# A GRU step on one core: candidate scan into PSUM, bank zeroings in steps of their own, keep's high products later

## What is computed

```python
def step(hprev, gxt):
    gh = hprev @ whh.T + bhh
    r = jax.nn.sigmoid(gxt[:, :h] + gh[:, :h])
    z = jax.nn.sigmoid(gxt[:, h:2 * h] + gh[:, h:2 * h])
    n = jnp.tanh(gxt[:, 2 * h:] + r * gh[:, 2 * h:])
    hn = (1.0 - z) * n + z * hprev
    return (hn, hn)
...
fwd = _bigru(x_inner, f_wih_fw, f_whh_fw, f_bih_fw, f_bhh_fw, f_wih_rv, f_whh_rv, f_bih_rv, f_bhh_rv)
bwd = jnp.flip(_bigru(jnp.flip(x_inner, 1), b_wih_fw, b_whh_fw, b_bih_fw, b_bhh_fw, b_wih_rv, b_whh_rv, b_bih_rv, b_bhh_rv), 1)
y = jax.nn.silu(fwd + bwd) * jax.nn.silu(z)
```

## Time and profile before

| | |
|---|---|
| median of 3 runs | 1226.55 us (1225.07 to 1228.66) |
| the profiled execution | 1223.94 us |
| its span | 1222.1 us |
| steps of L2, first to last reset product of `h_hi` | 296.4 to 722.0 us |
| PE, DVE, ACT busy | 1081.0, 943.3, 777.5 us |
| mean granted TensorE clock | 0.585 |
| ACT zeroings of a bank half | 120 of `reset_sum`, 120 of `keep_sum` in both layers |

### The profile page before, as it was taken

How to read it: one execution, slowest core, us unless ns; L and a number is a source line. 1 busy time by engine, 2 the same in 40 slices (tenths; PEclk the granted TensorE clock), 3 DMA queues, 4 the chain that set the end, 5 groups by cost and what they waited for, 6 DMA issues and landing times. The chain is left out here.

```text
span 1222.1 us, 57375 instructions
## 1 busy us (share of the span) xinstructions
PE 1081.0 (88%) x22390; PEld 854.9 (70%) x22390; DVE 943.3 (77%) x5701; ACT 777.5 (64%) x4509; POOL 113.1 (9%) x94
## 2 busy tenths in 40 slices
PE   3787799858999999999999968999999999999996
PEld 2555254344888888888888855688888888888885
DVE  3544799984888888888888885688888888888886
ACT  4224620007777777777777764777777777777773
POOL 1001389910000000000000000000000000000000
PEclk8588899957555555555555557555555555555555
DMA  4000500000000000000000000000000000000000
GB/s 119 2 1 12 131 1 1 1 5 2 4 4 4 4 4 4 4 4 4 3 4 4 4 3 5 3 4 4 3 4 4 4 4 3 4 4 4 4 3 27
DMA packets 8234, 12.71 MB, mean 10 GB/s; under 512 B 5745, under 2 KB 7121, under 8 KB 7674
## 3 DMA queue, kind: packets, MB, share of 16 engines
q1 hardware_dynamic: 7962, 9.05, 2.9%
HBM read 8.26 MB, written 0.79 MB: 7 GB/s over the span
## 5 line engine op out<-in xcount | busy, mean ns | idle before, releaser
L1037 DVE TENSOR_TENSOR_SCAN L2s_h_hi<-L2s_renew,L2s_terms 96x32 f16<-96x32 f32 x512 | 112.9, 221 | 74.4 <-ACT L2s_terms L1081 16.0
L1037 DVE TENSOR_TENSOR_SCAN L3s_h_hi<-L3s_renew,L3s_terms 96x32 f16<-96x32 f32 x512 | 113.0, 221 | 74.4 <-ACT L3s_terms L1081 16.0
L1129 PE MATMUL L2s_reset_sum<-L2s_h_hi,L_w_hidden 97*128 97x8 f16 x2048 | 141.0, 179 | 20.8 <-DVE L2s_h_hi L1037 8.4
L1129 PE MATMUL L3s_reset_sum<-L3s_h_hi,L_w_hidden 97*128 97x8 f16 x2048 | 141.1, 179 | 20.6 <-DVE L3s_h_hi L1037 7.8
L1129 PEld LDWEIGHTS L3s_reset_sum<-L3s_h_hi,L_w_hidden 97*128 97x128 f16 x2048 | 94.6, 107 | 78.6 <-DVE L3s_h_hi L1037 31.5
L1129 PEld LDWEIGHTS L2s_reset_sum<-L2s_h_hi,L_w_hidden 97*128 97x128 f16 x2048 | 94.6, 107 | 78.6 <-DVE L2s_h_hi L1037 32.0
L1072 ACT ACTIVATE L3s_reset<-L3s_reset_sum 96x16 f32<-96x16 f32 x512 | 93.0, 182 | 65.8 <-PE L3s_reset_sum L1129 5.1
L1072 ACT ACTIVATE L2s_reset<-L2s_reset_sum 96x16 f32<-96x16 f32 x512 | 93.0, 182 | 65.7 <-PE L2s_reset_sum L1129 4.6
L1081 ACT ACTIVATE L2s_terms<-L2s_cand 96x16 f32<-96x16 f32 x512 | 111.0, 217 | 30.1 <-DVE L2s_cand L1022 3.5
L1129 PE MATMUL L3s_keep_sum<-L3s_h_hi,L_w_hidden 97*128 97x8 f16 x2048 | 130.0, 174 | 0.0
L1129 PE MATMUL L2s_keep_sum<-L2s_h_hi,L_w_hidden 97*128 97x8 f16 x2048 | 130.0, 174 | 0.0
(11 more groups left out here) (251 smaller groups left out, 3415.2 us busy)
## 6 DMA issues: line engine op xcount, KB each, us to landing
L_wih_raw<-in_L_wih SPq DMA_DIRECT2D x2, 1152.0 KB, 11.6
l_w_raw<-in_L_w SPq DMA_DIRECT2D x1, 1296.0 KB
L_w_hidden_raw<-in_L_whh SPq DMA_DIRECT2D x2, 576.0 KB
stream<-in_x SPq DMA_DIRECT2D x2, 384.0 KB, 3.7
out<-stream SPq DMA_DIRECT2D x4, 192.0 KB, 2.1
l_idft<-in_idft SPq DMA_DIRECT2D x1, 400.0 KB
rpe_lw<-in_rpe_lw SPq DMA_DIRECT2D x1, 384.0 KB
l_dft<-in_dft SPq DMA_DIRECT2D x1, 288.0 KB, 3.0
```

Source lines behind the costliest of these rows:

```text
L1037: e.tensor_tensor_scan(flat(h_hi[g][0:C, x]), flat(renew[g][:, x]), flat(terms[g][:, x]), 0.0, ALU.mult, ALU.add).then_inc(hi_ready[g], 1)
L1129: return e.matmul(dst, weights.hidden[0:rows, wp, GATES * (2 * g + j) + gate, :], rhs, start=False, stop=False, skip_group_check=True)
```

## The change

Three edits, all in `gru_steps`:

1. `cand`, the result of the candidate scan, moves from an SBUF buffer to unused columns of the PSUM bank `cand_sum` of the same group and parity (row 2 of its four). The scan writes it there, and the tanh reads it there.
2. Of the two zeroings of a group only one stands in a step. Those of `reset_sum` are in step 0 (group 0) and 1 (group 1), those of `keep_sum` in step 2 and 3. The products ahead for reset begin one step behind its zeroing, as do those for keep.
3. Keep's four high products move from ahead of the wait for `lo_ready` to behind the candidate's low products.

```diff
         each = lambda n: [sem(f"{n}{g}") for g in range(GROUPS)]
         bank = lambda n: ctx.enter_context(nc.psum_tensor(f"{layer}s_{n}", [P, 4, PER, STEPS], F32))
         reset = pairs("reset", [C, 2, PER, 2])
-        cand = pairs("cand", [C, 2, PER, 2])
         keep = pairs("keep", [C, 2, PER])
         renew = pairs("renew", [C, 2, PER, 2])
         terms = pairs("terms", [C, 2, PER, 2])
@@ -985,6 +984,8 426.42 0.22 ACT L1081 ACTIVATE L2s_terms<-L2s_cand 96x16 f32<-96x16 f32 x1
...
426.58 0.17 DVE L1029 TENSOR_TENSOR L2s_terms<-L2s_keep,L_states 96x16 f32<-96x16 f32 x1
...
426.85 0.22 DVE L1037 TENSOR_TENSOR_SCAN L2s_h_hi<-L2s_renew,L2s_terms 96x32 f16<-96x32 f32 x1
         reset_sum = lambda g, p: reset_bank[g][:, p]
         keep_sum = lambda g, p: keep_bank[g][:, p]
         cand_sum = lambda g, p: cand_bank[g][p][:, 0:2].rearrange("p a c s -> p (a c) s").rearrange("p (c k) s -> p c k s", k=2)
+
+        cand = lambda g, p, x: cand_bank[g][p][0:C, 2].rearrange("p c s -> p (c s)")[:, x * 2 * PER:(x + 1) * 2 * PER]
         warm = sb("warm", [C, 1])
         prepared = sem("prepared")
 
@@ -992,6 +993,8 426.42 0.22 ACT L1081 ACTIVATE L2s_terms<-L2s_cand 96x16 f32<-96x16 f32 x1
...
426.58 0.17 DVE L1029 TENSOR_TENSOR L2s_terms<-L2s_keep,L_states 96x16 f32<-96x16 f32 x1
...
426.85 0.22 DVE L1037 TENSOR_TENSOR_SCAN L2s_h_hi<-L2s_renew,L2s_terms 96x32 f16<-96x32 f32 x1
         activated, cand_ready = each("activated"), each("cand_ready")
         updated, hi_ready, lo_ready = each("updated"), each("hi_ready"), each("lo_ready")
         PREPARED = 2 + 7 * GROUPS
+
+        RESET_ZEROED, KEEP_ZEROED = (0, 1), (2, 3)
 
         with nc.Block() as block:
 
@@ -1019,7 +1022,7 426.42 0.22 ACT L1081 ACTIVATE L2s_terms<-L2s_cand 96x16 f32<-96x16 f32 x1
...
426.58 0.17 DVE L1029 TENSOR_TENSOR L2s_terms<-L2s_keep,L_states 96x16 f32<-96x16 f32 x1
...
426.85 0.22 DVE L1037 TENSOR_TENSOR_SCAN L2s_h_hi<-L2s_renew,L2s_terms 96x32 f16<-96x32 f32 x1
                     x = q % 2
                     e.wait_ge(activated[g], 3 * q + 1)
                     e.wait_ge(cand_summed[g], q + 1)
-                    e.tensor_tensor_scan(flat(cand[g][:, x]), flat(reset[g][:, x]), flat(cand_sum(g, p)[0:C, :, :, s]), 0.0,
+                    e.tensor_tensor_scan(cand(g, p, x), flat(reset[g][:, x]), flat(cand_sum(g, p)[0:C, :, :, s]), 0.0,
                                          ALU.mult, ALU.add).then_inc(cand_ready[g], 1)
 
                 def kept_part(g, q):
@@ -1065,7 +1068,7 426.42 0.22 ACT L1081 ACTIVATE L2s_terms<-L2s_cand 96x16 f32<-96x16 f32 x1
...
426.58 0.17 DVE L1029 TENSOR_TENSOR L2s_terms<-L2s_keep,L_states 96x16 f32<-96x16 f32 x1
...
426.85 0.22 DVE L1037 TENSOR_TENSOR_SCAN L2s_h_hi<-L2s_renew,L2s_terms 96x32 f16<-96x32 f32 x1
                 for q in range(SEQ):
                     p, s = q // STEPS % 2, q % STEPS
                     x = q % 2
-                    renewed = s == 0 and 1 <= q // STEPS < CHUNK_COUNT - 1
+                    renewed = 1 <= q // STEPS < CHUNK_COUNT - 1
                     for g in range(GROUPS):
 
                         e.wait_ge(reset_summed[g], q + 1)
@@ -1073,12 +1076,13 426.42 0.22 ACT L1081 ACTIVATE L2s_terms<-L2s_cand 96x16 f32<-96x16 f32 x1
...
426.58 0.17 DVE L1029 TENSOR_TENSOR L2s_terms<-L2s_keep,L_states 96x16 f32<-96x16 f32 x1
...
426.85 0.22 DVE L1037 TENSOR_TENSOR_SCAN L2s_h_hi<-L2s_renew,L2s_terms 96x32 f16<-96x32 f32 x1
                         e.wait_ge(keep_summed[g], q + 1)
                         e.activation(keep[g][:, x], keep_sum(g, p)[0:C, :, s], ACT.Sigmoid).then_inc(activated[g], 1)
                         e.activation(renew[g][:, x, :, 1], keep_sum(g, p)[0:C, :, s], ACT.Sigmoid, scale=-1.0)
-                        if renewed:
+                        if renewed and s == RESET_ZEROED[g]:
                             e.activation(reset_sum(g, 1 - p)[0:C], zeros[:], ACT.Copy)
+                        if renewed and s == KEEP_ZEROED[g]:
                             e.activation(keep_sum(g, 1 - p)[0:C], zeros[:], ACT.Copy)
 
                         e.wait_ge(cand_ready[g], q + 1)
-                        e.activation(terms[g][:, x, :, 0], cand[g][:, x, :, 1], ACT.Tanh).then_inc(activated[g], 1)
+                        e.activation(terms[g][:, x, :, 0], cand(g, p, x).rearrange("p (c k) -> p c k", k=2)[:, :, 1], ACT.Tanh).then_inc(activated[g], 1)
 
             @block.tensor
             def _(e):
@@ -1135,18 +1139,22 426.42 0.22 ACT L1081 ACTIVATE L2s_terms<-L2s_cand 96x16 f32<-96x16 f32 x1
...
426.58 0.17 DVE L1029 TENSOR_TENSOR L2s_terms<-L2s_keep,L_states 96x16 f32<-96x16 f32 x1
...
426.85 0.22 DVE L1037 TENSOR_TENSOR_SCAN L2s_h_hi<-L2s_renew,L2s_terms 96x32 f16<-96x32 f32 x1
                                     run(product)
 
                         e.wait_ge(hi_ready[g], q + 1)
-                        for gate in (RESET, CAND, KEEP):
+                        def high(gate):
                             for j in range(2):
                                 add(gate, 0, 0, j)
                                 add(gate, 1, 0, j)
-                        ahead(RESET, 1)
+
+                        high(RESET)
+                        high(CAND)
+                        ahead(RESET, RESET_ZEROED[g] + 1)
 
                         e.wait_ge(lo_ready[g], q + 1)
                         add(RESET, 0, 1, 0)
                         add(RESET, 0, 1, 1).then_inc(reset_summed[g], 1)
                         add(CAND, 0, 1, 0)
                         add(CAND, 0, 1, 1).then_inc(cand_summed[g], 1)
-                        ahead(KEEP, 1)
+                        high(KEEP)
+                        ahead(KEEP, KEEP_ZEROED[g] + 1)
                         add(KEEP, 0, 1, 0)
                         add(KEEP, 0, 1, 1).then_inc(keep_summed[g], 1)
                         ahead(CAND, 0)
```

## The result

The changed kernel takes 1229.96 us (median of 20 runs, 1227.15 to 1234.57), the kernel before 1226.81 (20 runs, 1223.43 to 1228.97). The ratio is 1.0037, with a 95% interval of 1.0026 to 1.0048: slower by 3 to 6 us. The forecast was 1219.9, a gain. The profiled execution of the changed kernel took 1229.85 us. (In the diff of the change above, the rows with times behind six of the `@@` marks, 426.42 to 426.85, are those of the earlier trace rows and no part of the edit.)

The account below looks back on a forecast made before the run. Chain 1 was taken to bound the kernel, tied with chain 2 within 0.01. Zeroings -10.8 and late keep +4.1 gave -6.7 us, so 1226.55 became 1219.9 us; range 1213 to 1231.

Parts of the forecast that it names:

- Chain 1: One slot long: candidate scan, h_lo of the other group, low products, reset sigmoid, next scan; 0.81 us, without slack.
- ordinary slot: One group of one step, undisturbed, from reset sigmoid to reset sigmoid; 0.81 us, expected to stay so.
- chain 2: Two slots long: scan, tanh, h_hi, high products, product ahead, low products, reset sigmoid, scan; 1.62 us, tied within 0.01.
- Keep's four products: On PE, behind the candidate's low products: low products reached 0.11 earlier, ordinary slot saves 0, keep gets late.
- slots with two products: Slots with two of keep's products ahead, three per chunk: each delays its group's next slot about 0.03; 4.1 us lost.
- Each zeroing in a slot of its own: On ACT, 120 pairs become 240 single zeroings, taken as hidden with tanh at 0.56; 10.8 us saved.
- chain 3: Inside DVE: h_hi, state scan 0.14 later, next scan 0.12 behind; 0.05 to spare before, a tie in zeroed slots.
- Tanh from PSUM: On ACT, the tanh reading PSUM instead of SBUF is 0.04 shorter, on the two-slot chain alone.
- The write into PSUM: Candidate scan on DVE writing PSUM: taken as 0; a longer hold would cost 1.024 us per ns, at most 38 us.
- irregular late slots: Late slots making up the rest between 0.81 and 0.833 us per slot; left as they are.
- The first rival: From scan to h_lo, writing PSUM holds DVE longer: slower by over 0.3% from 11 ns, 1258 us at 37; chance 0.18.
- the read side: DVE scans reading PSUM hold DVE 0.11 against 0.12 from SBUF: reading costs nothing, so writing was taken as 0.

Follow-up runs that it names:

- Kernel 4: The kernel before with only keep's high products moved behind the candidate's low ones; 1231.24 us, ratio 1.0040.
- kernel 3: The kernel before with only the candidate scan writing PSUM and the tanh reading it there; 1233.82 us, ratio 1.0067.
- kernel 1: The changed kernel with the candidate scan writing SBUF again and the tanh reading it there; 1226.61 us, ratio 1.0004 to the kernel before.
- kernel 2: The kernel before with only the zeroings split over four steps, products ahead starting a step behind them; 1214.79 us, ratio 0.9914.
- kernel 5: The changed kernel with keep's high products back in their old place; 1227.59 us, ratio 1.0005 to the kernel before.

## Why the prediction was wrong

Point by point, in its own steps.

- **What bounds the kernel: right.** Chain 1 alone sets the ordinary slot. Kernel 4 shortened chain 2 by 0.11 and the slot stayed 0.81; kernel 3 lengthened h_lo, in chain 1, by 12 ns and the mean ordinary slot followed with 13.
- **Keep's four products, saving nothing in the ordinary slot: right.** H_hi is due 0.75 and 0.81 after the reset sigmoid with one and two products ahead, forecast as 0.75 and 0.80. The cost was put at 4.1 us from slots with two products. The places are as forecast (behind group 1 at step 4, shared with group 0 at step 5, and behind step 7). The size is 0.04 in kernel 1, where the slot is 0.81, against 0.033 forecast, but 0.014 in the changed kernel, whose slots are longer anyway: a late scan does not wait, and its h_lo then ends about 285 ns after the scan's start in either memory, so those slots never pay for PSUM.
- **Each zeroing in a slot of its own, 10.8 us: right.** 10.3 us alone (kernel 2). In the changed kernel tanh is at 0.56 and h_hi at 0.77, as worked out. The tie in chain 3 fails with a tanh of 0.21 (kernel 1) and holds with one of 0.18. That it holds is partly luck: the longer slot of the changed kernel gives chain 3 0.014 more than the forecast had, and no kernel has the late keep and the short tanh with a slot of 0.81.
- **Tanh from PSUM, 0.04 shorter: right**, 181 against 217 ns.
- **The write into PSUM, taken as 0: the step that failed.** Its text named two effects, a later end of the scan that "delays the tanh only", and a longer hold of DVE. The hold is unchanged, and the scan ends 8 ns later, both as it had them. Missed was that the end of the next instruction moves with it. That instruction is h_lo, the one place where a nanosecond costs 1.024 us. Measured 12 ns on h_lo and 13 to 14 on the slot. The rows of before could have warned: the start-to-start distance was used for the cost of an instruction to its successor, while PE waits for the successor's end, and no row of DVE had a successor of a write into PSUM.
- **The sum.** With the measured parts: -10.3 for the zeroings (kernel 2), +13.5 for the ordinary slot, +3.0 for the late keep, and -0.6 for the irregular late slots, which stand out less where the ordinary slot is longer (9.4 us in kernel 2, 8.8 in kernel 5). That is 5.6 us, and the steps show 5.7; it is 5.9 between the two profiled executions and 3.2 between the medians. The first rival was the right one, in place (from the scan to h_lo, chain 1) and in price: 1.024 us per ns, slower by over 0.3% from 11 ns on. It had 0.18. Its mechanism was stated as a longer hold, which did not happen.
- **The range.** It ended at 1231 and the median lies inside it; the direction was wrong. The chances put 0.65 on faster on the strength of the read side alone.

The rows of the changed kernel put the cost of the write at 14 ns per slot. The prediction set aside what the Trainium skill says (Perfetto Trace Analysis, Optimizing Scalar/DVE Operations): a DVE instruction pays about 125 ns on PSUM and about 60 on SBUF. An estimate from these figures is 65 ns per slot: the trace agrees with the sign, which was the better guide here, and not with the size.

## What to carry to other kernels

In a recurrence, price an instruction by the end that its consumer waits for, not only by when it lets the next one start; a change to one instruction can move the end of the one behind it. An operand may be moved to the memory that is nearer to its reader only if the writer's side, its successor included, is off the chain; here 36 ns saved on a chain with slack cost 12 ns on h_lo, and 13 to 14 on the slot, in the chain without. And of several edits made together measure each alone: the split zeroings were worth 0.9% and were hidden by the other two.

## What was not expected of the hardware

- A DVE scan of 96x32 writing PSUM lasts 224 ns against 216 into SBUF, and a subtraction of 96x16 behind it 158 against 146, with the start-to-start distance unchanged; with nothing else running the same.
- If the scan did not have to wait, h_lo behind it ends at the same time whichever memory the scan writes, 0.28 to 0.29 after the scan's start (0.11 + 0.17, and 480.29 to 480.40 with 0.17 above; medians 284 ns before and 285 ns changed).
- ACT's tanh of 16 columns: 217 ns from SBUF, 181 from PSUM.
